# The last sequence's probabilities are turned on TensorE instead of by DMA; two waits on FFN weights move within the second step

## What is computed

```
h = tok(x)                                   # q + softmax(q k) v over t, (64, 128, 192)
h = h + attn(layernorm(h), Wq, Wk, Wv, Wo)   # 12 heads of 64, 3 kv heads, rope
h = h + ffn(layernorm(h))                    # 192 -> 768, gelu, 768 -> 192

# inside attn, for every sequence and head
scores = einsum('bhqd,bhkd->bhqk', q, k) * SCALE
attn = softmax(scores)
out = einsum('bhqk,bhkd->bhqd', attn, v)
return out @ Wo
```

## Time and profile before

| | |
|---|---|
| median of 3 runs | 1038.31 us (1038.16 to 1040.47) |
| profiled execution, its own time | 1040.1 us |
| its span in the trace | 1038.1 us |
| PE busy | 999.2 us, 96% of the span |
| DVE, ACT, POOL busy | 811.2, 731.5, 435.1 us |
| mean granted TensorE clock | 0.993 |

### The profile page before, as it was taken

How to read it: one execution, slowest core, us unless ns; L and a number is a source line. 1 busy time by engine, 2 the same in 40 slices (tenths; PEclk the granted TensorE clock), 3 DMA queues, 4 the chain that set the end, 5 groups by cost and what they waited for, 6 DMA issues and landing times. The chain is left out here.

```text
span 1038.1 us, 24559 instructions
## 1 busy us (share of the span) xinstructions
PE 999.2 (96%) x7274; PEld 862.3 (83%) x7274; DVE 811.2 (78%) x2095; ACT 731.5 (70%) x2532; POOL 435.1 (42%) x585
## 2 busy tenths in 40 slices
PE   7879999999999999999999999999999999999996
PEld 4668888888888888888888889888888888888875
DVE  3777888877888887888887788787788888778861
ACT  4548677677777667777767877767777766786761
POOL 0343454444444444344444345444434443434540
PEclk9989999999999999999999999999999999999999
DMA  5233443443453443344343444344345434344431
GB/s 176 82 111 109 135 144 110 132 124 106 129 149 120 118 139 111 117 141 137 102 146 116 115 129 149 118 119 132 110 117 149 127 110 143 111 120 135 124 105 45
DMA packets 139935, 127.49 MB, mean 123 GB/s; under 512 B 30992, under 2 KB 123024, under 8 KB 139920
## 3 DMA queue, kind: packets, MB, share of 16 engines
q1 hardware_dynamic: 137056, 124.05, 40.3%
q10 hardware_dynamic: 2864, 3.26, 1.0%
HBM read 70.63 MB, written 56.62 MB: 123 GB/s over the span
## 5 line engine op out<-in xcount | busy, mean ns | idle before, releaser
L421 POOL TENSOR_TENSOR E<-E,e_rcp 128x512 f32<-128x512 f32 x192 | 198.4, 1040 | 288.5 <-DVE e_rcp L561 285.4
L306 ACT ACTIVATE E<-ring,m_neg 128x128 f32<-128x128 f32 x768 | 272.1, 389 | 57.0 <-DVE m_neg L541 57.0
L413 POOL TENSOR_TENSOR q_tok<-rot_c,rot_s 128x384 f32<-128x384 f32 x128 | 125.6, 1001 | 128.7 <-DVE rot_s L519 128.7
L306 ACT ACTIVATION_READ_ACCUMULATOR E<-ring,m_neg 128x1 f32 x768 | 174.8, 228 | 0.0
L541 DVE TENSOR_REDUCE m_neg<-ring 128x4 f32<-128x512 f32 x192 | 122.5, 681 | 53.9 <-PE ring L758 53.9
L300 ACT COPY qkT<-ring 128x512 f32<-128x512 f32 x128 | 71.9, 588 | 128.4 <-PE ring L734 128.4
L552 DVE STREAM_TRANSPOSE EB<-E 128x512 f32<-128x512 f32 x192 | 134.2, 699 | 17.6 <-POOL E L421 17.5
L893 PE MATMUL ring<-wo_sb,OT 128*128 128x192 f32 x756 | 139.9, 335 | 1.4 <-ACT OT L314 1.4
L744 PE MATMUL bank<-wout_sb,G 128*128 128x192 f32 x720 | 126.9, 326 | 0.0
L893 PEld LDWEIGHTS ring<-wo_sb,OT 128*128 128x128 f32 x756 | 122.6, 192 | 4.7 <-issue 2.0
L744 PEld LDWEIGHTS bank<-wout_sb,G 128*128 128x128 f32 x720 | 117.6, 190 | 0.1
(11 more groups left out here) (148 smaller groups left out, 2298.4 us busy)
## 6 DMA issues: line engine op xcount, KB each, us to landing
spill<-EB SPq DMA_DIRECT2D x64, 512.0 KB, 2.7
ET<-spill SPq DMA_DIRECT2D x256, 128.0 KB, 2.8
spill<-EB SPq DMA_DIRECT2D x64, 256.0 KB, 2.1
ET<-spill SPq DMA_DIRECT2D x256, 64.0 KB, 2.4
x_sb<-in_x_dram SPq DMA_DIRECT2D x64, 192.0 KB, 2.5
out_dram<-out_sb SPq DMA_DIRECT2D x64, 96.0 KB, 2.3
x_sb<-in_x_dram SPq DMA_DIRECT2D x64, 64.0 KB, 2.3
w_raw<-in_w_att_dram ACTq DMA_DIRECT2D x2, 576.0 KB, 4.4
```

The source lines that it names most:

```text
L306: last = nc.scalar.activation(E[:, a, s * P:(s + 1) * P], RING[a][:, s * P:(s + 1) * P], ACT.Exp, bias=m_neg[:, a, s:s + 1], accum_out=e_s ...
L413: nc.gpsimd.tensor_tensor(q_tok[:, a, c], rot_c[:, a, c], rot_s[:, a, c], ALU.add).then_inc(q_out, 1)
L421: nc.gpsimd.tensor_tensor(e, e, r, ALU.mult).then_inc(prob_out, 1)
```

## The change

1. In step 31 (NP-1), for a = 1 alone, DVE no longer turns 32x32 blocks and SP no longer moves them (two writes and eight reads gone). PE turns the twelve heads itself, four to a bank (`last_probs_turned`), into B7, `RING[1][:, 0:512]` and B7 again; DVE copies each bank to ET (`probs_copied`). `probs_v(1)` now follows in step 31, and writes to `RING[0]`; DVE copies its result to OT (`last_heads_out`), where ACT did. `output(0)` now stands behind `probs_v(1)`, and `output(1)` follows it, into a bank of its own (`LAST_Y`, in B7).
2. Step 32 loses `probs_v(1)`, `output(1)` and one `kept_warm`.
3. In step 1 PE's waits on `s_lo` and `s_dup` stand at the start of `ffn_first` instead of the start of the step.

```diff
+        LAST_T, LAST_Y = (B7[:], RING[1][:, 0:512], B7[:]), B7[:, 0:D]
...
             def step(p, att, ffn, fin, more):
-                if ffn:
+                if ffn and not (isinstance(p, int) and p == NP):
                     blocks_moved(1, p - 1)
...
-                if ffn:
+                if ffn and not (isinstance(p, int) and p == NP):
                     heads_out(1, p - 1)
...
+                def probs_copied(k):
+                    g = GROUPS[k]
+                    s0, heads = PIECES[g // 2]
+                    h0 = REP * g - s0
+                    dve.wait_ge(last_mm, k + 1)
+                    nc.vector.tensor_copy(
+                        ET[:, 1, s0 * P:(s0 + heads) * P].rearrange("p (i h c) -> p h i c", i=NB, h=heads)[:, h0:h0 + REP],
+                        LAST_T[k].rearrange("p (h i c) -> p h i c", h=REP, i=NB)).then_inc(last_out, 1)
...
-                if att:
+                if att_last:
+                    sums_inverted(1, 1, p)
+                    sums_inverted(1, 2, p)
+                    for k in range(3):
+                        probs_copied(k)
+                    last_heads_out()
+                elif att:
                     sums_inverted(1, 1, p)
                     blocks_turned(1, 0, p)
...
+                def last_probs_turned(k):
+                    g = GROUPS[k]
+                    pe.wait_ge(prob_out, 6 * p + 3 + k + 1)
+                    if k == 2:
+                        pe.wait_ge(last_out, 1)
+                    for h in range(REP):
+                        c = slice((REP * g + h) * P, (REP * g + h + 1) * P)
+                        last = nc.tensor.transpose(LAST_T[k][:, h * P:(h + 1) * P], E[:, 1, c], ident[:])
+                    last.then_inc(last_mm, 1)
...
+                    if first == "ffn":
+                        pe.wait_ge(s_lo, 4)
+                        pe.wait_ge(s_dup, 1)
                     pe.wait_ge(HL_out, p)
...
-                if first == "ffn":
-                    pe.wait_ge(s_lo, 4)
-                    pe.wait_ge(s_dup, 1)
...
-                if ends and ffn:
-                    kept_warm(1, RING[0])
-                if ffn:
+                if ffn and not ends:
                     probs_v(1, p - 1)
...
+                if att_last:
+                    for k in range(3):
+                        last_probs_turned(k)
+                    last_pair = True
+                    probs_v(1, p)
                 if att:
                     output(0, p)
+                if att_last:
+                    output(1, p)
```

More of the change, by code:

```diff
@@ L181, in program @@
         pv_mm, OT_out = sem("pv_mm"), sem("OT_out")
+        last_mm, last_out, last_OT = sem("last_mm"), sem("last_out"), sem("last_OT")
         y_mm, h2_out, h2_copied = sem("y_mm"), sem("h2_out"), sem("h2_copied")
@@ L497, in step @@
                 att_first = isinstance(p, int) and p == 0
+                att_last = isinstance(p, int) and p == NP - 1
                 def x_lo():
@@ L564, in attention_added @@
                     dve.wait_ge(y_mm, done)
-                    nc.vector.tensor_tensor(h2[:, a, :], ATT_Y0 if att_first and a == 0 else ATT_Y, h_cur[:, a, :], ALU.add).then_inc(h2_out, 1)
+                    y = ATT_Y
+                    if att_first and a == 0:
+                        y = ATT_Y0
+                    if a == 1 and not att:
+                        y = LAST_Y
+                    nc.vector.tensor_tensor(h2[:, a, :], y, h_cur[:, a, :], ALU.add).then_inc(h2_out, 1)
                 def attention_stats(a, done):
@@ L682, in step @@
                     ffn_lo()
+                if att and not att_last:
+                    blocks_turned(1, 2, p)
                 if att:
-                    blocks_turned(1, 2, p)
                     dve.wait_ge(h_kept, p + 1)
@@ L703, in step @@
                 ends = isinstance(p, int) and p >= NP
+                last_pair = False
+                att_last = isinstance(p, int) and p == NP - 1
                 def kept_warm(count, bank=B6):
@@ L767, in probs_v @@
                         pe.wait_ge(tqk_out, n + 1)
+                    ring = RING[a]
+                    if a == 1 and last_pair:
+                        ring = RING[0]
+                        pe.wait_ge(OT_out, 4 * q + 2)
                     first_8 = ET[:, a, 0:8 * P].rearrange("p (i h c) -> p i h c", i=NB, h=8)
@@ L887, in output @@
                         pe.wait_ge(exp_out, 6 * q + 6)
+                    elif last_pair:
+                        pe.wait_ge(last_out, 3)
                     else:
                         pe.wait_ge(h2_out, 2 * q + 1)
+                    y = ATT_Y0 if first == "att" else ATT_Y
+                    if a == 1 and last_pair:
+                        y = LAST_Y
                     for t in range(6):
-                        if t % 4 == 0:
+                        if t % 4 == 0 and a == 1 and last_pair:
+                            pe.wait_ge(last_OT, t // 4 + 1)
+                        elif t % 4 == 0:
                             pe.wait_ge(OT_out, 4 * q + 2 * a + t // 4 + 1)
-                        last = nc.tensor.matmul(ATT_Y0 if first == "att" else ATT_Y, OT[:, a, t * P:(t + 1) * P], wo_sb[:, t, :],
+                        last = nc.tensor.matmul(y, OT[:, a, t * P:(t + 1) * P], wo_sb[:, t, :],
                                                 start=(t == 0), stop=(t == 5))
```

14 lines of the change are left out of this document (12 added, 2 removed).

## The result

| | before | changed |
|---|---|---|
| median | 1038.31 us (5 runs, 1038.01 to 1040.7) | 1033.57 us (5 runs, 1031.89 to 1034.97) |
| ratio | | 0.9942, 95% interval 0.9925 to 0.9959 |
| profiled execution | 1040.1 us | 1031.89 us |
| its span | 1038.1 us | 1029.9 us |
| its mean granted clock | 0.993 | 0.998 |

The medians say 4.7 us, the ratio 6.0 (4.3 to 7.8), the two profiled executions 8.2. The forecast was 6.7, to 1031.6 us; the measured median is 2.0 above that and inside the range. The three sizes of one gain already say that something else moves by several microseconds from one execution to the next.

The account below looks back on a forecast made before the run. The prediction took PE, busy for 96% of the span, to bound the loop, leaving only the edges. The end's 5.9 us and the start's 0.8 sum to 6.7, from 1038.3 to 1031.6 us; range 1028.8 to 1034.8 us.

Parts of the forecast that it names:

- The bound and the two places: Loop bound by PE; gains left at step 1's FFN-weight wait (3.9 us) and step 32's exchanged-block wait (3.75 us).
- The end, steps 1 to 8: PE's queue rebuilt from the last `probs_v(0)` to `ffn_first` of step 32, which starts 1020.6 instead of 1026.5: 5.9 us gained.
- Step 7: Ahead of `hn_turned` in step 32: `hn` is ready at 1018.0, 0.5 us ahead of PE, a thin cover.
- the forecast's chain: At the end, DVE's first and third copies of turned probabilities, 0.68 us each, lie on the path to `probs_v(1)`.
- The clock in the old end: Low clock over the old `output(1)`: 1.5 us of the end's gain; another execution may meet 0.5 to 1.5 us elsewhere.
- The start: Step 1 with moved weight waits: PE arrives 1.9 us earlier, less 1.1 of low clock; `scores(0)` ends 0.8 us earlier.
- Rival D: Start edit gives nothing or costs up to 0.5 us, end gives 5 us: 1033.3 to 1034.5 us; chance 0.06.
- B: At the end, the clock falls behind the new transposes; 3.4 us at half clock cost 1.7: 1033.3 us; chance 0.10.
- C: Start gains 1.9 us instead of 0.8, clock not falling or falling late, and end 6.0: 1030.4 us; chance 0.13.
- E: Slower than before: DVE's copies into 32-wide pieces take 2.1 us and up each; 1040.2 us at 2.5; chance 0.02.
- F: Moved waits do not act, or the loop's 29 iterations lose 4.4 us in another rhythm: 1036.0 us; chance 0.05.
- the last of the forecast's signs of being wrong: The distance from `scores(0)` of step 1 to the loop's last iteration is not that of before.

## Why the prediction was right, and where it was not

**The bound and the two places.** Right. The loop was bound by PE before and is still.

**The end, steps 1 to 8.** Right, and nearly in its times. Counted from the start of `probs_v(0)`:

| | forecast | changed kernel |
|---|---|---|
| third group of transposes | 2.8 | 2.97 |
| `probs_v(1)` | 3.5 | 3.57 |
| `output(0)` | 4.9 | 5.01 |
| `hn_turned` | 13.2 | 13.56 |
| `ffn_first` | 15.3 | 15.56 |

The gain was sized at 5.9 us and measured at 5.67 against the first trace of before. The missing 0.2 lie in small waits ahead of `output(0)` (0.1) and in `hn_turned`, whose first matmul began 0.80 us behind the first weight load of `kept_warm` (1015.55) where the forecast had 0.6. The copy of 512 columns, taken at 0.68 between bounds of 0.35 and 1.05, takes 0.68 or 0.69. Step 7, the thin cover of 0.5 us, was right: `hn` is ready at 1015.67 and PE comes 0.7 later, 0.6 of which can be had. The doubled copies added 1.44 us, within the 1.4 to 2.1 of the forecast's chain over the first and the third copy, and do not tell it from a chain over all three. The own bank's 0.8 us was named and not priced.

**The clock in the old end.** Right in kind. Three traces of the old end give 28.94, 29.71 and 29.87, so its low clock, of 6.8 us in the longer two and 3.4 in the first, costs up to 0.9 us more than in the one trace that the forecast had. Their mean less 23.28 is 6.2 us, which fits the 6.3 of the end's edit by its ratio.

**The start.** This is the term that was wrong. It was sized at 0.8 us, as 1.9 of earlier arrival less 1.1 of low clock, with 0.1 to 1.7 (to -0.5). Measured, the edit alone is 1.000 (0.999 to 1.0009), so between +0.9 and -1.0 us. Its path held: DVE's rotation waits for nothing of PE, and the clock falls in the new gap. Two steps failed. The first is the base: 9.57 us from F2S to `scores(0)` was taken as what the old waits cost, but their three traces give 8.89 to 9.94; in all three the low clock ended ahead of `tok_vq`, and the lowest has 3.4 us of it over `qkv(0)` where the others have 6.8. The forecast let the clock vary in the new order and held it fixed in the old one. The second is where the new low clock lies. The forecast let `tok_vq` arrive 1.9 us earlier, 6.32 us behind F2S, and counted the low clock from there on. At full clock it does arrive at 6.40 (62.99 - 56.59, with the products of zeros), but in the changed kernel the clock was low over the q and k transposes already, and it came at 6.89, 1.3 us earlier than the 8.19 of before. The low stretch then covered most or all of `tok_vq` in all eight traces with moved waits and nothing in the gap (1.49 us for its first product in each), and the scores began 1.2 to 1.8 us later than at full clock; the forecast had put 1.1 in the middle of 0.2 to 1.8. Rival D had this mechanism, with 0.06, which was too little. Moving a wait leaves PE's idle time as long as it was when another engine's chain sets what comes behind, and then the low clock falls on the next work instead of on `qkv`.

**From the profile to the median.** The forecast took 6.7 us off the median. The profiled pair shows 8.2, of which 1.27 stem from a low stretch that the trace of before had in step 0 and that of after had not. The medians moved 4.7 us, and the ratios of the changed kernel's two sets of runs 6.0 and 5.2. The measured median lies inside the range although the start's 0.8 us did not come: the range is 6 us wide, and a term of that size is lost in it. Only the edits run apart show it.

**Rivals.** B (the clock falls behind the transposes) did not occur in any of the eleven traces that have them (clock 1.00 from 1005 to 1028 us in each). C (the start gives the full 1.9) needed the products of zeros, and with them gave 1.2 to 1.8. E is excluded by the copies' 0.69 us. F: the moved waits act, and nothing of 4.4 us was lost in the loop. But the last of the forecast's signs of being wrong was met: from `scores(0)` of step 1 to the last `probs_v(0)` it took 939.88 us before and 939.22 in the changed kernel. The edits did not bring that about, for the same kernel shows both lengths. From the `HH` cast of step 2 to that of step 31, 29 iterations, it takes 889.4 to 889.6 us in eight of the fourteen traces and 890.1 to 890.3 in six. The two traces of the changed kernel gave 889.4 and 890.1, those of the kernel before 890.2 and 890.1. PE's waits for POOL's rotated queries between 100 and 980 us are 5.0 or 5.1 us in the eight and 5.4 to 5.6 in the six, so most of the 0.7 lies there. The changed kernel's, beside the earlier trace rows:

```profile
PE ring L768 <- POOL q_tok L415: 5.0, 29, 0.2
```

Why an execution takes the one length or the other stays open. Two prices of the rivals do not follow from their own terms: five copies at 2.5 us and not 0.68 add 9.1 to 1031.6, so 1040.7 and not E's 1040.2, and 5 us gained less 0.5 lost is 1033.8, not D's 1034.5. Neither decides anything.

## What to carry to other kernels

Before booking a wait as a gain, follow the chain of the engine that will be late next. Here PE waited 3.9 us, but DVE and POOL decided when it could go on, and the wait only moved. When PE must be idle at an edge, the place of the wait matters less than the clock behind it: 2.6 us of products of zeros in the gap brought `scores(0)` 1.2 to 1.8 us forward where the moved wait brought nothing. Then look further on: in two of three traces a later low stretch took part of it back. An exchange by DMA on the last item of a pipeline has nothing left to hide under; with it, 13.8 us went by from the end of POOL's last product to the end of `output(1)`, and 6.7 us do with the turning on TensorE, though `output(0)` now stands in between.

## What was not expected of the hardware

48 transposes in a row (5.24 us of PE's queue) kept the granted clock at 1.00. And the clock of the first 80 us is a draw: the two traces of the kernel before have 10.2 and 20.5 us of low clock there, and the 17 runs of the same kernel had mean clocks of 0.987 to 0.996 and spans of 1034.0 to 1040.1 us on one chip, the fastest at 0.996 and the slowest at 0.987. One trace of such a kernel shows one draw, and a start or an end has to be compared by its own stretch, from an event that no edit moves, in more than one trace.
